# Two attention layers with experts between them on one core: unrolled experts, halved stores, a second DMA queue, sums in PSUM

## The chip, the cores and the metric

One core of a Trainium2 chip runs the whole program in one launch. The metric is the device time of an execution in microseconds (us). PE is TensorE, DVE VectorE, ACT ScalarE, POOL GpSimd and SP SyncE.

## The reference

Four layers follow each other, each added to its input and then normalised over 128 features:

```
x = layernorm(x + attention0(x))   # 16 x 256 tokens, 16 heads of 64, a window mask
x = layernorm(x + experts(x))      # 16 experts 128 -> 512 -> 128, gelu, the best 4 per token, softmax weights
x = layernorm(x + attention1(x))   # 16 heads of 8, weights plus a rank-16 correction
x = layernorm(x + gates(x))        # c = f*c + i*g over the 16 batches, h = tanh(x wo + c_final uo + bo)
```

The gated recurrence runs over the batches, so its last state c_final is known only at the end, and every output row needs it.

## The kernel before, in words

**First attention** (to 667 us). A batch has 256 tokens in two tiles and eight steps `p`. A batch's normalised rows `x1c` are scattered one batch later to a DRAM table `xs`, sorted by expert, by eight indirect DMAs that POOL issues, two per step; the row numbers `pos` come from a chain of small DVE operations behind the routing.

**Experts.** 144 tiles of 128 sorted rows. For each, SP loads rows (`xg<-xs`), PE turns them and multiplies by `wA`, ACT applies gelu, PE multiplies by `wB`, DVE adds the bias, and SP stores to `ys`. 24 tiles make a turn; the first two turns and the last stand written out, three run in a loop. The semaphore `a_done` holds all engines at the start until each has ended the first attention.

**Second attention.** Iteration `b` works on several batches at once: scores and softmax of batch b, score maxima for b+1, queries and keys for b+2, normalisation for b+3, fetches of expert results (`yk<-ys`, eight indirect DMAs per batch, POOL) for b+5, gates for b-2. Queries and keys are split into three bf16 parts; SP stores them (`qkd<-parts`), and reads them back as ten loads, in rows of 4096 bf16 (8 KB), the stack `qst`/`kst` (one of three stacks lies in `wall`, so that loads show as `wall<-qkd`). Row maxima of the first 8 heads are ready at step 5, of the other 8 at step 1 of the next iteration: PE turns them, ACT copies them to `mrow`, SP copies `mrow` eight times into the stack (`qst<-mrow`, `wall<-mrow`, L459). PE's transposed scores (L892) of steps 0 and 4 wait for the two copies. Then ACT takes exponentials (L1086) from one pair of PSUM tiles, PE multiplies with the values (L904).

**End.** When the last state is known PE forms c_final uo (L994), DVE and POOL add it and `bo2` to all 16 batches' outputs in SBUF (L1477, L677), ACT takes tanh (L1151), then four groups of eight tiles are summed, normalised and stored, the last scaling on ACT (L1156).

The order on each engine is that in which the code is written; PE, for example, takes the score products (`scores`) of step 7 after turning the next batches' rows.

Of the kernel before, what the change touches and what calls it, by code (L numbers as in the profile page):

```python
# [10 lines left out]
ALU = mybir.AluOpType  # L11
# [18 lines left out]
GT = 128  # L30
# [3 lines left out]
TURN = 24  # L34
# [67 lines left out]
def build(nc, t, out):  # L102
    ctx = ExitStack()
    with ctx:
# [3 lines left out]
        def sem(name):  # L108
# [147 lines left out]
        state = sb("state", [128, TT, D])  # L256
# [15 lines left out]
        qkd = nc.dram_tensor("qkd", (2, NPART, 128, N), bf16, kind="Internal").ap()  # L272
# [7 lines left out]
            ksq_ready rmat_ready a_done plan_ready zrow_ready plan_out plan_in filled  # L280
# [3 lines left out]
            yk_in0 yk_in1 gates_in weighed comb_done var2_ready pow2_ready posc_ready state_mm state_ready h_pre h_pre_last last_sum var3_ready pow3_ready scale_ready h_act fin_ready out_done""".split()  # L284
# [26 lines left out]

        def group(c):

            return [x[:, 8 * c:8 * c + 8, :].rearrange("q (k i) d -> q k i d", i=TT) for x in (xo_all, x_all)]

        def per_batch(v):
            return v[:, :, :].rearrange("q (o i) d -> q o i d", o=1).to_broadcast([128, 4, TT, D])
# [41 lines left out]
        def _(sp):  # L359
# [39 lines left out]
            sp.wait_ge(s["a_done"], 4)  # L399

# [14 lines left out]

            for n in range(4):
                load_rows(n, n)
# [8 lines left out]
            batch_loop(sp, 2, NT // TURN - 1, 2, body)  # L426
# [3 lines left out]
            def attention(b, par):  # L430
                if has(b, 0):
                    spread_maxima(b, TMB, par, 1)
                if has(b, 2):
                    load = (par + 2) % 3
                    need_alone(sp, "parts_ready", b + 3)

                    need_alone(sp, "stk", 16 * NSTK * (b + 2))
                    for w in range(2):
                        sp.dma_start(qkd[w].rearrange("a r n -> r a n"), parts[:, :, w * N:(w + 1) * N]).then_inc(s["qkd_out"], 16)
                    need_alone(sp, "qkd_out", 32 * (b + 3))  # L440

                    need_alone(sp, "st_full", 8 * b)
                    rows = qkd.rearrange("w a (d h) n -> w (a d) h n", h=H1)
                    n = 0
                    for qa in range(NPART):
                        count = NPART - qa
                        sp.dma_start(kst[load][DH1 * n:DH1 * (n + count), :, :], rows[1, 0:DH1 * count, :, :]).then_inc(s["stk"], 16)
                        for k in range(count):
                            sp.dma_start(qst[load][DH1 * (n + k):DH1 * (n + k + 1), :, :], rows[0, DH1 * qa:DH1 * (qa + 1), :, :]).then_inc(s["stk"], 16)
                        n += count  # L450
                    sp.dma_start(qst[load][MROW:MROW + NMAX, :, :], no_maxima).then_inc(s["stk"], 16)
                if has(b, 1):
                    spread_maxima(b, TMA, (par + 1) % 3, 0)

            def spread_maxima(b, use, slot, half):

                need_alone(sp, f"free{use[0]}", tally[use[0]].before(b, use[1] + 1))
                hh = H1 // 2
                sp.dma_start(qst[slot][MROW:MROW + NMAX, half * hh:half * hh + hh, :],  # L459
                             mrow[:, half, :].rearrange("q (o n) -> q o n", o=1).to_broadcast([NMAX, hh, N])).then_inc(s["mrow_in"], 16)  # L460

            no_maxima = zeros.bitcast(bf16).rearrange("(q h) n -> q h n", h=H1)
# [3 lines left out]
            for c in range(B // 4):  # L466
                sp.wait_ge(s["fin_ready"], c + 1)
                sp.dma_start(out[c * 4 * N:(c + 1) * 4 * N, :].rearrange("(n p) d -> p n d", p=128), x_all[:, 8 * c:8 * c + 8, :]).then_inc(s["out_done"], 16)
            sp.wait_ge(s["out_done"], 16 * B // 4)

        @block.gpsimd
        def _(pool):
# [25 lines left out]
            def body(b):  # L498
                for p in range(8):
# [3 lines left out]
                    if p == 4 and is_batch(b, -1):  # L503
# [3 lines left out]
                    if p == 5 and is_batch(b, -1):  # L507
                        need(pool, "x1c_ready", b)
                        g.tensor_copy(x_all[:, bass.ds((b - 1) * TT, TT), :], x1c[:, :, :]).then_inc(s["x1_kept"], 1)
                    if p < 4 and is_batch(b, -2):  # L510
# [3 lines left out]
                        for k in (2 * p, 2 * p + 1):  # L514
                            nc.gpsimd.indirect_dma_start(  # L515
                                out=xs, out_offset=bass.IndirectOffsetOnAxis(pos[:, k:k + 1], 0),
                                in_=x1c[:, k // TOPK, :], in_offset=None).then_inc(s["scat"], 16)
# [84 lines left out]
            def fetch(b, par, half):  # L602

                if has(b, 5):
                    slot, count = (par + 2) % 3, TT * TOPK // 2
                    need_alone(pool, f"yk_in{half}", 16 * count * (b + 5))
                    if half == 0:
                        need_alone(pool, "comb_done", b + 3)
                        g.tensor_copy(gcur[:, slot, :], gate_all[:, bass.ds(b + 5, 1), :].rearrange("q o k -> q (o k)")).then_inc(s["gates_in"], 1)
                    first = bass.ds((b + 5) * TT * TOPK + count * half, count)  # L610
                    g.tensor_copy(posc[:, half, :], pos_all[:, first]).then_inc(s["posc_ready"], 1)
                    need_alone(pool, "posc_ready", 2 * (b + 5) + (half + 1))
                    for n in range(count):
# [32 lines left out]
            def new_state(b):  # L646

                if has(b, -2):
# [7 lines left out]
                    g.tensor_tensor(c2[:, :], c2[:, :], tg[:, :], ALU.add).then_inc(s["scan_done"], 1)  # L656

# [9 lines left out]
            for b in range(-5, 2):  # L667
                outputs(b, b % 3)
# [6 lines left out]
            xo, xt = group(GROUPS - 1)  # L675
            pool.wait_ge(s["state_ready"], 1)
            g.tensor_tensor(xo, xo, per_batch(state), ALU.add).then_inc(s["h_pre_last"], 1)  # L677
            for c in range(GROUPS):
                if c == 1:
                    pool.wait_ge(s["h_act"], GROUPS)  # L680
                    g.tensor_tensor(xt, xt, xo, ALU.add).then_inc(s["last_sum"], 1)
# [4 lines left out]
        def _(pe):  # L686
# [125 lines left out]
            def after_attention(b, p):  # L812

                if p == 5:
# [3 lines left out]
                    for it in range(TT):  # L818
                        last = nc.tensor.transpose(M[:, it * 128:(it + 1) * 128], x1c[:, it, :], ident[:, :])
# [23 lines left out]
            pe.wait_ge(s["a_done"], 4)  # L843
# [10 lines left out]
            rows_in(1, 1, 16)  # L854
            def tiles(i):
                for p in range(TURN):
                    n, two = TURN * i + p, p % 2
                    if is_tile(i, p, 0):
# [3 lines left out]
                        for f in range(FC):  # L862
                            at = (f // 2) * 512 + (f % 2) * GT
                            mm(UP[two][:, at:at + GT], wA[:, p % 4, f * 128:(f + 1) * 128], xgT[:, p % 4, :], start=True, stop=True).then_inc(s["up_mm"], 1)  # L864
                    if is_tile(i, p, 2):
# [10 lines left out]
            batch_loop(pe, 2, NT // TURN - 1, 2, tiles)  # L876
# [5 lines left out]
            def attention(b, par):  # L882
                nxt = (par + 1) % 3
                for p in range(8):
# [22 lines left out]
                    if p == 4 and has(b, -2):  # L907
                        need(pe, "scan_done", b - 1)
                        need_x2T_x3T(pe, b)
                        gates(b, GA)  # L910
                    if p == 6 and has(b, -2):
# [26 lines left out]
                    if p == 3 and has(b, -1):  # L938
# [4 lines left out]
                        last.then_inc(s[f"full{WO[0]}"], 1)  # L943
                    if p == 7 and (has(b, 3) or has(b, -1)):
# [11 lines left out]
                    scores(b, p, nxt)  # L956
# [32 lines left out]

            attention_loop(pe, attention)  # L990
# [566 lines left out]
```

## Time and profile before

| | |
|---|---|
| median of 3 runs | 1532.71 us (1528.11 to 1534.6) |
| profiled execution | 1530.1 us, of which the span of its instructions is 1528.3 us |
| mean granted clock of TensorE | 0.93 |
| PE busy | 1270.1 us (83% of the span) |
| DVE, ACT, POOL busy | 1011.6, 939.1, 796.6 us |

Times in rows are us from the start of the span. A row of the timeline is start, length, engine, line of the code, operation, `out<-in`, shape and number of instructions merged; in brackets stands how long the engine was idle before it and what ended that. The granted clock is 1.0 for 2.4 GHz and 0.5 for 1.2 GHz.

### The profile page before, as it was taken

The numbers are of one execution on the slowest core, as the hardware profiler recorded it, in microseconds if no ns is written. First come the engines' busy times: TensorE is split into PE (matmuls) and PEld (weight loads), VectorE is DVE, ScalarE is ACT, GpSimd is POOL, SyncE is SP. The second block draws the span as 40 slices with busy tenths as digits, with TensorE's granted clock in tenths as the row PEclk, the third lists the DMA queues.
The fourth block names the chain that finished last, engine by engine and source line by source line (L and its number), as shares of the span: only waits on it lengthen the run. The fifth ranks groups of instructions, "written<-read, shape, count | busy, mean of one in ns | idle before, by whom it ended". The sixth has DMA issues, their size and how long they took to land.

```text
span 1528.3 us, 36861 instructions
## 1 busy us (share of the span) xinstructions
PE 1270.1 (83%) x9712; PEld 970.9 (64%) x9712; DVE 1011.6 (66%) x3751; ACT 939.1 (61%) x2828; POOL 796.6 (52%) x1025
## 2 busy tenths in 40 slices
PE   7999999999999999856999889803768787878870
PEld 3776767777777776646999889801445554555540
DVE  2677777777777777755776657514677776668726
ACT  5877777777777777624665456412555655656544
POOL 1557777777777777743332100175456665653133
PEclk9999999999999999978999999955899999999995
DMA  9522222222222222112222122115343435343201
GB/s 345 171 60 70 69 67 67 69 69 69 69 69 69 69 69 69 44 51 58 72 69 70 58 61 70 56 45 92 82 86 74 94 66 91 68 88 57 46 4 55
DMA packets 150448, 115.51 MB, mean 76 GB/s; under 512 B 11809, under 2 KB 139937, under 8 KB 148290
## 3 DMA queue, kind: packets, MB, share of 16 engines
q1 hardware_dynamic: 142146, 97.50, 24.9%
q0 software_dynamic: 8192, 16.79, 4.2%
q8 instruction: 39, 0.64, 0.2%
q14 instruction: 71, 0.58, 0.1%
HBM read 50.02 MB, written 61.08 MB: 73 GB/s over the span
## 4 chain that ended last, share of the span: by engine, by line
PE 29%; DMA 7%; DVE 5%; issue 4%; DVEq 3%; POOL 2%; ACT 2%; another core or an unknown queue 2%; SPq 1%; POOLq 1%; ACTq 0%
PE psum L864 8%; PE psum L873 8%; DMA qst<-mrow 3%; DMA wall<-mrow 3%; PE psum L904 2%; PE psum L892 2%; PE psum L967 2%; POOL yk L614 1%; PE psum L983 1%; PE psum L850 1%; DVE mx L1389 1%; PE psum L984 1%; ACT wall L1086 1%; DMA yk<-ys,posc 1%
## 5 line engine op out<-in xcount | busy, mean ns | idle before, releaser
L525 POOL TENSOR_SCALAR P<-P,rinv 128x192 f32<-128x192 f32 (+1 forms) x384 | 309.4, 820 | 154.1 <-DVE rinv L1216 151.7
L1051 ACT ACTIVATE P<-shifted,least 128x192 f32<-128x192 f32 (+1 forms) x512 | 240.2, 471 | 103.2 <-DVE least L1202 101.8
L1076 ACT ACTIVATE hid<-psum,wA 128x128 f32<-128x128 f32 x576 | 164.7, 369 | 118.9 <-PE psum L864 118.9
L1389 DVE TENSOR_REDUCE mx<-psum 128x2 f32<-128x512 f32 x256 | 165.0, 686 | 83.4 <-PE psum L967 56.1
L1086 ACT ACTIVATE wall<-psum 128x1024 f32<-128x1024 f32 x128 | 131.1, 1024 | 98.9 <-PE psum L892 81.7
L1202 DVE CUSTOM_DVE_ANT_0 shifted<-psum,band 128x192 f32<-128x192 f32 (+1 forms) x512 | 168.7, 384 | 26.0 <-PE psum L749 25.7
L864 PE MATMUL psum<-xgT,wA 128*128 128x128 f32 x1152 | 155.8, 279 | 8.9 <-DVE xgT L1355 8.8
L515 POOL DMA_INDIRECT xs<-x1c,pos x128 | 128.2, 1001 | 56.8 <-issue 28.3
L873 PE MATMUL psum<-wB,hid 128*128 128x128 f32 x1152 | 153.5, 277 | 0.0
L614 POOL DMA_INDIRECT yk<-ys,posc x128 | 124.2, 970 | 55.7 <-issue 29.0
L864 PEld LDWEIGHTS psum<-xgT,wA 128*128 128x128 f32 x1152 | 143.4, 196 | 9.6 <-issue 9.5
L873 PEld LDWEIGHTS psum<-wB,hid 128*128 128x128 f32 x1152 | 141.5, 194 | 0.0
L786 PEld LDWEIGHTS psum<-ident,P 128*128 128x128 f32 x1024 | 117.0, 141 | 36.3 <-issue 29.4
L786 PE MATMUL psum<-ident,P 128*128 128x128 f32 x1024 | 134.9, 274 | 3.7 <-POOL P L525 1.5
L749 PE MATMUL psum<-kT,qT 64*128 64x192 f32 (+1 forms) x1024 | 131.5, 375 | 0.6 <-DVE least L1202 0.6
L804 PE MATMUL psum<-PT,V 128*64 128x256 f32 (+1 forms) x1024 | 112.2, 362 | 0.7 <-DVE PT L1190 0.7
L749 PEld LDWEIGHTS psum<-kT,qT 64*128 64x128 f32 x1024 | 80.2, 186 | 38.6 <-issue 36.9
L1348 DVE COPY wA<-wall 128x516 f32 x144 | 61.9, 430 | 64.4 <-ACT hid L1076 41.5
L1051 ACT ACTIVATION_READ_ACCUMULATOR P<-shifted,least 128x1 f32 x512 | 95.9, 187 | 0.0
L1190 DVE COPY PT<-psum 128x448 f32<-128x448 f32 x128 | 79.0, 618 | 17.1 <-PE psum L804 7.8
L697 PE MATMUL psum<-hT,wg 128*128 (+1 forms) x256 | 88.9, 429 | 1.7 <-ACT kT L1008 0.9
L804 PEld LDWEIGHTS psum<-PT,V 128*64 128x64 f32 x1024 | 68.5, 138 | 30.9 <-issue 9.0
(243 smaller groups left out, 2550.7 us busy)
## 6 DMA issues: line engine op xcount, KB each, us to landing
xs<-zrow SPq DMA_DIRECT2D x33, 1024.0 KB
xg<-xs SPq DMA_DIRECT2D x144, 64.0 KB, 1.8
ys<-yrow SPq DMA_DIRECT2D x72, 128.0 KB, 1.9
wall<-in_wall SPq DMA_DIRECT2D x1, 8232.0 KB, 36.5
qkd<-parts SPq DMA_DIRECT2D x32, 192.0 KB
qst<-qkd SPq DMA_DIRECT2D x66, 64.0 KB
wall<-qkd SPq DMA_DIRECT2D x35, 64.0 KB
kst<-qkd SPq DMA_DIRECT2D x11, 192.0 KB
```

The costliest lines, as they stand in the source:

```text
L525: g.tensor_scalar(x, x, rinv[:, par, n:n + 1], None, ALU.mult).then_inc(s["pn_ready"], 1)
L614: g.indirect_dma_start(out=yk[:, slot, count * half + n, :], out_offset=None, in_=ys, in_offset=bass.IndirectOffsetOnAxis(posc[:, half, n: ...
L749: last = mm(bk[:, c0:c0 + w], qT[64 * h:64 * h + 64, p, it * 128:(it + 1) * 128], kT[64 * h:64 * h + 64, p, 0:w], start=True, stop=True)
L786: last = nc.tensor.transpose(bk[:, c0:c0 + 128], P[:, par1, it, h, jt * 128:(jt + 1) * 128], ident[:, :])
L804: last = mm(OTB[64 * h:64 * h + 64, k * N + c0:k * N + N], V[:, jt, r * 128 + 64 * h:r * 128 + 64 * h + 64], PT[:, k, h, keys], start=(jt ...
L864: mm(UP[two][:, at:at + GT], wA[:, p % 4, f * 128:(f + 1) * 128], xgT[:, p % 4, :], start=True, stop=True).then_inc(s["up_mm"], 1)
L873: last = mm(DN[two][:, 0:D], hid[:, m, f, :], wB[:, m, f * D:(f + 1) * D], start=(f == 0), stop=(f == FC - 1))
L1051: last = sc.activation(P[:, par, it, h, 0:w], shifted[:, par, it, h, 0:w], ACT.Exp, scale=-1.0, bias=least[:, par, n:n + 1], accum_out=row ...
L1076: sc.activation(hid[:, p % 4, f, :], UP[two][:, at:at + GT], ACT.Gelu, bias=wA[:, p % 4, F + f:F + f + 1]).then_inc(s["hid_ready"], 1)
L1086: sc.activation(pc[:, p % 4, :, :, :].rearrange("q h j n -> q (h j n)"), ST, ACT.Exp, scale=SCALE1).then_inc(s["exps1"], 1)
L1202: v.tensor_tensor_reduce(out=shifted[:, par, it, h, 0:w], in0=bk[:, c0:c0 + w], in1=band[:, it, 0:w], scale=-SCALE0, scalar=3.0e38, op0=AL ...
L1389: v.tensor_reduce(out=mx[:, :, h], in_=SB[(par + 1 + h) % 3].rearrange("q (i n) -> q i n", i=TT), axis=mybir.AxisListType.X, op=ALU.max).t ...
```

## The change

It joins five edits: the experts' turns are all written out (a turn is 8 tiles); the parts are stored by halves of 64 partitions, heads 0 to 7 and 8 to 15, and read back as two pieces of 4 KB per partition; the copies of maxima are issued by ACT; the last state is added on PE, in PSUM, where the outputs are put by a product with the identity; and several waits and orders between the stages are changed. The core of the diff:

```diff
-TURN = 24
+TURN = 8
+        def rows_of(b):
+            return h1[:, 0, :].rearrange("q (i d) -> q i d", d=D)[:, 0:TT, :] if isinstance(b, int) and b == B - 1 else x1c
...
-            sp.wait_ge(s["a_done"], 4)
+            first_rows = [row_of(n) for n in range(4)]
+            sp.wait_ge(s["scat"], 16 * B * TT * TOPK)
             for n in range(4):
-                load_rows(n, n)
+                sp.dma_start(xg[:, n, :], xs[bass.ds(first_rows[n], GT), :]).then_inc(s[f"xg_in{n}"], 16)
...
-            batch_loop(sp, 2, NT // TURN - 1, 2, body)
+            for i in range(NT // TURN + 1):
+                body(i)
...
                     for w in range(2):
-                        sp.dma_start(qkd[w].rearrange("a r n -> r a n"), parts[:, :, w * N:(w + 1) * N]).then_inc(s["qkd_out"], 16)
+                        for e in range(2):
+                            sp.dma_start(qkd[w, e].rearrange("a r n -> r a n"), parts[64 * e:64 * e + 64, :, w * N:(w + 1) * N]).then_inc(s["qkd_out"], 16)
...
-                    if p == 4 and is_batch(b, -1):
+                    if p == (3 if isinstance(b, int) and b == B else 4) and is_batch(b, -1):
                         need_alone(pool, "var_ready", b)
                         g.tensor_tensor(rstd[:, :], veps[:, :], minus_half[:, 0:TT], ALU.pow).then_inc(s["pow_ready"], 1)
...
+                if has(b, -2):
+                    need_alone(pool, f"free{GB[0]}", tally[GB[0]].before(b, GB[1] + 1))
+                    g.tensor_tensor(xo, xo, bo2[:, :].rearrange("q (o d) -> q o d", o=1).to_broadcast([128, TT, D]), ALU.add).then_inc(s["xo_kept"], 1)
...
+            fetch(-4, -4 % 3, 0, 0, 2)
+            combine(-4, -4 % 3)
+            fetch(-4, -4 % 3, 0, 2, 3)
+            deviations(-3)
...
+                    if p == 5 and isinstance(b, int) and b == B:
+                        outputs_in(0)
+                        outputs_in(1)
...
+                    scores(b, p, nxt)
                     if p == 7 and (has(b, 3) or has(b, -1)):
...
-                    scores(b, p, nxt)
...
             attention_loop(pe, attention)
             pe.wait_ge(s["scan_done"], B + 1)
-            for it in range(TT):
-                last = mm(SB[0][:, it * D:(it + 1) * D], c2[:, it * 128:(it + 1) * 128], gu[:, 3, :], start=True, stop=True)
+            state_in(0)
+            state_in(1)
+            outputs_in(3)
+            state_in(2)
+            state_in(3)
...
+            sc.activation(sqj[:, 0:1], ident[:, 0:1], ACT.Gelu)
...
             def maxima_row(b, use, slot, half):
                 need_full(act, b, use)
                 sc.activation(mrow[:, half, :], shared(use).bitcast(bf16)[0:NMAX, 0:N], ACT.Copy).then_inc(s[f"free{use[0]}"], 1)
+                need_alone(act, f"free{use[0]}", tally[use[0]].before(b, use[1] + 1))
+                act.dma_start(qst[slot][MROW:MROW + NMAX, half * hh:half * hh + hh, :],
+                              mrow[:, half, :].rearrange("q (o n) -> q o n", o=1).to_broadcast([NMAX, hh, N])).then_inc(s["mrow_in"], 16)
...
-                        need(dve, "scat", 16 * TT * TOPK * (b - 1))
+                        if not (isinstance(b, int) and b == B):
+                            need(dve, "scat", 16 * TT * TOPK * (b - 1))
...
+                    if p == 7 and isinstance(b, int) and b >= B:
+                        dve.wait_ge(s["gate_act"], b - 1)
+                        v.scalar_tensor_tensor(tf[:, :], tf[:, :], 1.0, c2[:, :], ALU.add, ALU.mult)
+                        v.scalar_tensor_tensor(tg[:, :], ti[:, :], 1.0, tg[:, :], ALU.add, ALU.mult)
+                        v.scalar_tensor_tensor(c2[:, :], tf[:, :], 0.5, tg[:, :], ALU.mult, ALU.add).then_inc(s["scan_done"], 1)
...
+                if c == GROUPS - 1:
+                    for k in range(4, 8):
+                        last = v.tensor_scalar(x, x, mv2[:, c, k, 0:1], rstd2[:, c, k:k + 1], ALU.subtract, ALU.mult)
```

Where the text above says heads by halves, the columns of `cwqk` are sorted likewise. On ACT the weighing of the fetched results of the first batches moves behind the first copy of `parts`.

**POOL, start of the second attention, before.** Behind the fetches for batch 0 stand four and four fetches for batch 1 around the sum of batch 0 (L640 to L644), and then the power for batch 0's deviation (L622):

```order
L614 DMA yk<-ys,posc 128x128 [waits posc_ready]
L614 DMA yk<-ys,posc 128x128 x3
L640 TENSOR_TENSOR yk<-yk 128x2x256 [waits weighed]
L642 TENSOR_TENSOR sums<-yk 128x256
L644 TENSOR_TENSOR sums<-sums,x_all 128x256
L611 COPY posc<-pos_all 128x4 [waits yk_in1]
L614 DMA yk<-ys,posc 128x128 [waits posc_ready]
L614 DMA yk<-ys,posc 128x128 x3
L622 TENSOR_TENSOR rstd<-ve,minus_half 128x2 [waits var2_ready]
```

The same place in the changed kernel:

```order
L611 DMA yk<-ys,posc 128x128 [waits posc_ready]
L611 DMA yk<-ys,posc 128x128
L637 TENSOR_TENSOR yk<-yk 128x2x256 [waits weighed]
L639 TENSOR_TENSOR sums<-yk 128x256
L641 TENSOR_TENSOR sums<-sums,x_all 128x256
L611 DMA yk<-ys,posc 128x128
L619 TENSOR_TENSOR rstd<-ve,minus_half 128x2 [waits var2_ready]
```

Three fetches instead of eight stand ahead of the power.

**ACT, step 5 of the last iterations of the second attention, changed kernel.** The copy to `mrow` is followed by the DMA, which waits until that copy is written (`free1`); before, the next exponential stood there:

```order
L1150 ACTIVATE wall<-psum 128x1024 [waits pv_full,st_full]
L1206 ACTIVATE mrow<-psum 24x256 [waits full1]
L1209 DMA qst<-mrow 24x8x256 [waits free1]
L1150 ACTIVATE wall<-psum 128x1024 [waits pv_full,st_full]
L1154 ACTIVATE oTc<-psum 128x256 [waits to_full,pv_full]
```

In the loop the weighing of fetched results (four activations) stands between the DMA and that exponential.

**PE, the end, before**, from the last gates (L983 with `x3T`, L984 with the state `c`) to the state's product:

```order
L983 MATMUL psum<-x3T,gw 128x256 [waits free1,free0,scan_done]
L984 MATMUL psum<-c,gu 128x256
L983 MATMUL psum<-x3T,gw 128x256
L984 MATMUL psum<-c,gu 128x256
L983 MATMUL psum<-x3T,gw 128x256 [waits free0]
L984 MATMUL psum<-c,gu 128x256
L987 MATMUL psum<-gw,x3T 128x128 x2
L994 MATMUL psum<-gu,c 128x128 [waits scan_done]
L994 MATMUL psum<-gu,c 128x128
```

and in the changed kernel:

```order
L1017 MATMUL psum<-x3T,gw 128x256 [waits free1,free0]
L1017 MATMUL psum<-x3T,gw 128x256 [waits free1]
L1017 MATMUL psum<-x3T,gw 128x256 [waits free0]
L1019 MATMUL psum<-gw,x3T 128x128 x2
L1041 MATMUL psum<-wall,ident 128x512 [waits o_free,to_free,max_done,xo_kept]
L1041 MATMUL psum<-wall,ident 128x512
L1023 MATMUL psum<-c,gu 128x256 [waits scan_done]
L1023 MATMUL psum<-c,gu 128x256 x2
L1048 MATMUL psum<-gu,c 128x2x128 [waits scan_done]
L1048 MATMUL psum<-gu,c 128x2x128 x7
L1041 MATMUL psum<-wall,ident 128x512 [waits free1,free0,xo_kept]
L1041 MATMUL psum<-wall,ident 128x512
```

The products with `x3T` now stand ahead of the wait for the state (`scan_done`), with one pair of identity products (L1041) between; four more such products stand earlier, between the gates of the batch before.

## Rows read from the trace of the kernel before

**Rows 1.** Second attention: length, busy PE, PEld, DVE, ACT, POOL, clock, DMA share, GB/s.

```profile
1068.00:1470.00 402.00, 320.81 (x2674) 213.29 (x2674) 282.01 (x854) 236.23 (x461) 202.96 (x275) 0.93 0.37 72
```

**Rows 2.** Timeline, PE, where the experts' loop returns to its start.

```profile
839.63 1.06 PE L873 MATMUL psum<-wB,hid 128*128 128x128 f32 x8
845.34 2.07 PE L864 MATMUL psum<-xgT,wA 128*128 128x128 f32 x8 [4.66 <-DVE xgT L1355]
...
897.23 1.93 PE L864 MATMUL psum<-xgT,wA 128*128 128x128 f32 x8 [4.10 <-DVE xgT L1355]
```

**Rows 3.** Timeline, DVE at the end of the first attention.

```profile
674.41 0.60 DVE L1262 TENSOR_SCALAR x1c<-res,mv,rstd 128x128 f32<-128x128 f32 x2 [0.52 <-DMA xs<-x1c,pos]
```

**Rows 4.** The chain that ended last, first attention to experts (start, length, what).

```profile
692.10 2.23 DMA xs<-x1c,pos
694.35 1.31 POOLq L529
697.90 1.69 DMA xg<-xs
```

**Rows 5.** Timeline, several engines, from the experts to the second attention.

```profile
1018.60 0.16 DVE L94 TENSOR_TENSOR u<-rstd 128x2 f32<-128x2 f32 x1 [5.26 <-POOL rstd L622]
...
1026.05 1.28 ACT L1136 ACTIVATE yk<-yk,gcur 128x128 f32<-128x128 f32 x4 [2.01 <-DMA yk<-ys,posc]
...
1030.87 0.38 SPq L447 DMA_DIRECT2D kst<-qkd  x1
...
1033.70 0.94 POOL L614 DMA_INDIRECT yk<-ys,posc  x1 [0.30 <-issue]
...
1043.62 1.28 ACT L1136 ACTIVATE yk<-yk,gcur 128x128 f32<-128x128 f32 x4 [16.29 <-DMA yk<-ys,posc]
1044.01 1.04 PE L967 MATMUL psum<-kst,qst 128*128 128x256 bf16 x4 [6.40 <-DMA qst<-zeros]
```

**Rows 6.** Line L459: issue (ns min/median/max) and who waited for it (us, times).

```profile
L459 SPq DMA_DIRECT2D qst<-mrow x22: 778/818/992, 1058.2 to 1456.6; - x22
...
  PE psum L892: 36.4, 10
```

**Rows 7.** Timeline, SP, ACT and PE, copies of maxima, second attention.

```profile
1067.94 1.04 PE L892 MATMUL psum<-qst,kst 128*128 128x256 bf16 x4 [6.90 <-DMA qst<-mrow]
...
1266.52 16.25 SPq L459 DMA_DIRECT2D wall<-mrow  x2
...
1274.27 1.02 ACT L1086 ACTIVATE wall<-psum 128x1024 f32<-128x1024 f32 x1 [1.06 <-remote]
...
1276.54 1.03 PE L892 MATMUL psum<-wall 128*128 128x256 bf16 x4 [2.65 <-DMA wall<-mrow]
1277.50 1.94 PE L904 MATMUL psum<-wall,v 128*32 128x256 f32 x16
...
1432.06 1.03 PE L892 MATMUL psum<-wall 128*128 128x256 bf16 x4 [4.93 <-DMA wall<-mrow]
...
1447.93 9.41 SPq L459 DMA_DIRECT2D qst<-mrow  x2
...
1452.84 0.60 PE L892 MATMUL psum<-qst,kst 128*128 128x256 bf16 x4 [0.33 <-ACT wall L1086]
```

**Rows 8.** Timeline, ACT, the exponential behind step 5's weighing.

```profile
1323.33 1.02 ACT L1086 ACTIVATE wall<-psum 128x1024 f32<-128x1024 f32 x1 [1.30 <-PE psum L892]
```

**Rows 9.** Timeline, the end.

```profile
1489.42 0.41 POOL L650 TENSOR_SCALAR tf<-tf 128x256 f32<-128x256 f32 x1 [5.75 <-ACT tg L1112]
...
1493.11 1.22 PE L994 MATMUL psum<-gu,c 128*128 128x128 f32 x4 [4.40 <-POOL c L656]
...
1498.36 4.28 ACT L1151 ACTIVATE wall<-wall 128x1024 f32<-128x1024 f32 x4 [8.85 <-DVE wall L1477]
1500.52 1.21 DVE L1484 TENSOR_TENSOR x_all<-x_all,wall 128x1024 f32<-128x1024 f32 x1
...
1518.43 6.26 ACT L1156 ACTIVATE x_all<-x_all,shift,rstd 128x128 f32<-128x128 f32 x16 [0.20 <-DVE shift L1493]
```

More of the change, by code:

```diff
@@ L310, in build @@
         GROUPS = B // 4
[L312 to L317, printed above, removed]
         def has(b, off):
@@ L646, in new_state @@
             def new_state(b):
-                if has(b, -2):
+                if has(b, -2) and not (isinstance(b, int) and b >= B):
                     need_alone(pool, "gate_act", b - 1)
@@ L874, in tiles @@
                         last.then_inc(s["dn_mm"], 1)
-            batch_loop(pe, 2, NT // TURN - 1, 2, tiles)
+            for i in range(NT // TURN + 1):
+                tiles(i)
             pe.wait_ge(s["c_set"], 1)
@@ L988, in gates, with last_gates @@
                 last.then_inc(s[f"full{use[0]}"], 1)
+            def last_gates(b):
+                need_x2T_x3T(pe, b)
+                parts = (GA, 0, 0), (GA, 1, 1), (GB, 0, 2)
+                for use, n, k in parts:
+                    need_free(pe, b, use)
+                    mm(shared(use)[:, n * N:(n + 1) * N], gw[:, k, :], x3T[:, :], start=(n == 0), stop=False)
+                for it in range(TT):
+                    mm(shared(GB)[:, N + it * D:N + (it + 1) * D], x3T[:, it * 128:(it + 1) * 128], gw[:, 3, :], start=False, stop=False)
+                outputs_in(2)
+                need(pe, "scan_done", b - 1)
+                for use, n, k in parts:
+                    last = mm(shared(use)[:, n * N:(n + 1) * N], gu[:, k, :], c2[:, :], start=False, stop=(n == 1 or use == GB))
+                    if n == 1 or use == GB:
+                        last.then_inc(s[f"full{use[0]}"], 1)
@@ L1076, in tiles @@
                             sc.activation(hid[:, p % 4, f, :], UP[two][:, at:at + GT], ACT.Gelu, bias=wA[:, p % 4, F + f:F + f + 1]).then_inc(s["hid_ready"], 1)
-            batch_loop(act, 2, NT // TURN - 1, 2, tiles)
+            for i in range(NT // TURN + 1):
+                tiles(i)
             def attention(b, par):
@@ L1125, in attention @@
                         last.then_inc(s[f"free{TX[0]}"], 1)
-                    if p == 7 and isinstance(b, int) and b == -3:
-                        for half in range(2):
-                            weigh(b, par, half)
             def weigh(b, par, half):
@@ L1341, in _ @@
             dve.wait_ge(s["plan_in"], 16)
+            dve.wait_ge(s["b2_kept"], E // 4)
             def expert_of(n):
@@ L1359, in _ @@
                 weights_A(first, n)
+                weights_B(first, n)
+            for n in range(2):
                 rows_T(n, n)
-                weights_B(first, n)
             def tiles(i):
@@ L1379, in tiles @@
                         weights_B(e, q)
-            batch_loop(dve, 2, NT // TURN - 1, 2, tiles)
+            for i in range(NT // TURN + 1):
+                tiles(i)
             def row_maxima(b, p, par):
```

196 lines of the change are left out of this document (111 added, 85 removed).

## Prediction

> **What bounds the kernel now.** I read the table of stretches, then the chain that ended last, then the timeline at each place that the change touches. PE is busy for 320.81 of the second attention's 402 us [rows 1], and for all but two gaps of the experts; the rest of the time is lost where a stage hands over to the next. Five places matter.
>
> *Experts' loop.* Tiles follow each other every 1.9 us, except that after the tile at 839.63 PE stands idle for 4.66 us and then multiplies at half clock (2.07 us instead of 1.06 for eight products); the same follows at 897.23 with 4.10 [rows 2]. Both places are the loop's return to its start.
>
> *First attention to experts.* The last rows are normalised at 674.41, after DVE has waited 0.52 us for the scatter of the batch before [rows 3]. The last scatter lands at 694.33, then comes POOL's drain (1.31) and the reading of row numbers, so that the second load of rows starts only at 697.90 [rows 4].
>
> *Experts to second attention.* POOL issues fetches at 1.24 us each (0.94 and 0.30 of idle). DVE waits 5.26 us for a power that stands behind them in POOL's order; the first stack of keys is loaded from 1030.87 on, and PE waits for its last part until 1044.01 [rows 5].
>
> *Second attention.* In ten iterations PE waits for the copy of maxima, 36.4 us in all [rows 6]. The copy issued at 1266.52 arrives at 1276.54, 10.0 us later; without stack loads around it the one of 1447.93 was there by 1452.84, so within 4.9 us [rows 7]. The burst of stack loads stands ahead of it in SP's queue.
>
> *End.* The state is ready at 1493.11, but DVE begins the first sum only at 1500.52, since the state is first added to all outputs, and ACT's last 16 scalings begin at 1518.43 and take 6.26 us [rows 9].
>
> **The change part by part**, against the profiled execution's own 1530.1 us, which is 0.17% under the median.
>
> *Experts written out.* Both gaps go: idle 4.66 and 4.10, and after each about two groups of eight products that took 1.01 and 0.87 us more than at full clock [rows 2]: 8.76 + 2.02 + 1.74 = 12.5. The turns that are already written out keep the 1.9 us beat, which is why I charge nothing for more code. Bounds: 11 (only the idle and one slow group each) to 13. **-12.5.**
>
> *To the experts.* The power for the last batch moves ahead of two scatters: 2 x 1.24 = 2.5, if a scatter costs what a fetch does. With a buffer of its own the last batch needs no wait for a scatter: 0.5 [rows 3]. Its `pos` is written ahead of three small operations: about 0.4. The eight last scatters thus start 3.4 earlier. Behind them SP waits for the scatters alone, with its row numbers read: between landing (694.33) and second load (697.90) lie 3.57 us [rows 4], of which I take 2.6, since the first load, which started earlier, is now what the first tile needs. The gelu table is loaded early, but PE hardly waited for it: nothing. Bounds 4.5 to 7. **-6.0.**
>
> *To the second attention.* Ahead of batch 0's power stand three fetches instead of eight: 5 x 1.24 = 6.2, and one copy of positions with its wait less, about 1. ACT does `parts` before it weighs the next batch. Against that SP issues two more stores: 0.5. The whole chain (power, x2T, queries, parts, stack) moves with it, since nothing else ends later than it there: PE had waited 6.40 us for the stack [rows 5]. Bounds 4 to 8.5. **-6.7.**
>
> *Second attention, copy of maxima.* Two prices are unknown. First, what a queue of its own saves. Nothing is the one end; the other is that the copy then takes 4.9 us or less, as without loads, and all removable waiting goes. Not all 36.4 are removable: at 1276.54 ACT had ended the exponential before only at 1275.29, so 1.2 of the 2.65 could go; read in the same way all ten (from 6.9 at 1067.94 to 4.7 of 4.93 at 1432.06) come to 26.5 [rows 6, 7]. Also, seven of the nine later waits are followed by scores at 1.03 instead of about 0.6 us and by L904 at 1.94 instead of about 1.1 [rows 7]: half clock, 1.4 us each, up to 9.8. Between the ends the nearest row is POOL's: the fetch issued at 1033.70, in a queue of its own, beside a burst of stack loads, was used only at 1043.62, 9.9 us later, when the loads ended too; ACT waited 16.29 us for it, and 2.01 for the one fetched ahead of the burst [rows 5]. So a queue of its own gave next to nothing while pieces were 8 KB. Pieces of 4 KB let another queue in twice as often, if queues take turns; I take a quarter of the way from 10.0 to 4.9, some 1.2 us per copy: 11.1 over the ten (two waits allow less), and two half-clock starts avoided: 2.8.
>
> By the Trainium skill (DMA: Bandwidth & Descriptors, "Queues, rings and completion order") SP and ACT have rings of their own on the same 16 DMA engines, and an engine goes round between the rings packet by packet; the fetch above, which shared no queue with the loads and yet ended with them, agrees with the shared engines, and no run here shows the size of a turn.
>
> Second, what an issue costs on ACT. SP's took 0.82 us in the median [rows 6], and ACT must also wait for its own write. At step 5 ACT stood idle for 1.30 us before the next exponential [rows 8], which covers an issue and a short wait; where that idle is not there, the exponential is late, and PE's next L892 with it. I take 0.2 us of each of 32 issues: 6.4. Bounds: nothing, and 32 x 0.82 = 26.2. POOL's addition of `bo2` and the moved scores I count at nothing: POOL is idle for half of this stretch (202.96 of 402 busy [rows 1]), and if that cover were gone, the next fetch would be late, needed a batch later. The SP queue loses its waits for ACT, but these hid nothing: it waits for `parts` next. **-11.1 - 2.8 + 6.4 = -7.5.**
>
> *End.* Up to the state I see no gain: DVE's three steps replace POOL's five (1489.42 to 1493.11, 3.7 us [rows 9]) twice, but six identity products come in on PE around the last gates. After it, PE must add the state to one group: L994's two products took 1.22 us at half clock, four of twice the width some 3.4 (estimate); with one tanh (4.28/4 = 1.07 [rows 9]) DVE starts 4.6 instead of 7.4 us after the state: -2.8. DVE scales four of the last 16 tiles, so ACT's last stretch falls from 6.26 to 4.7; DVE's part overlaps: -1.3. Bounds +1 (identity products on the path) to -8. **-4.1.**
>
> Sum: -12.5 - 6.0 - 6.7 - 7.5 - 4.1 = -36.8, so 1530.1 - 36.8 = **1493 us**.
>
> **Rivals.**
> 1. *The queue of its own gives nothing*: the copy still lands with the burst, as POOL's fetch did, while ACT pays 6.4. The second attention comes out at +6.4 instead of -7.5: 1507 us. For it: rows 5; against it: the shorter pieces.
> 2. *It frees the copy*: 26.5 and most of 9.8 us go, less 6.4: about -29 instead of -7.5: 1472 us. For it: 4.9 us without loads [rows 7]; against it: rows 5.
> 3. *Slower*: ACT's issue holds exponentials. All other terms give 43.2; to lose that over 32 issues each must expose 1.35 us, so more than the whole 0.82 that SP needs. To be slower by 8 us it must be 1.6: 1538 us. Only a far longer issue on ACT does that; no row speaks for it.
> 4. *The gaps are not the loop's*: if code that is fetched anew made them, they would stay, and 12.5 are lost: 1505 us. Against it: the written-out turns show none.
>
> The Trainium skill (same page, "Rules for kernel authors") says that spreading DMAs over issuing engines doesn't help bandwidth, and that two transfers to halves of the partitions aren't worth it; that is rival 1, 1507 us, and the fetch of rows 5 agrees with it so far.
>
> **How the numbers follow.** Forecast (1484 to 1500) 0.42, rival 2 with values up to it 0.24, rival 1 with 4 0.26, rival 3 0.03, no or hardly any change 0.05. The range reaches from a little under rival 2 (1467) to a little over rival 1 (1512). A measurement of this kernel tells about 0.5% (8 us) from no change: rivals 1, 2 and 4 all lie beyond it, so faster 0.92, same 0.05, slower 0.03.
>
> **What would show it.** Experts: no PE idle over 2 us between 705 us and the end of the tiles, 1.9 us per tile. To the experts: first load some 6 us earlier, no SP wait on POOL's drain. To the second attention: from the end of the experts to the first stack's use 7 us less. Copy of maxima: from ACT's issue to the waiting L892 about 8.8 us; 10 is rival 1, 5 is rival 2; idle of ACT ahead of step 6's exponential near zero. End: from the last state to DVE's first sum under 5 us. The prediction falls if the second attention as a whole (402 us) changes by over 20 us either way, or if the gaps at the tiles stay.

## The result, and the profile after

| | before | after |
|---|---|---|
| median | 1531.7 us | 1512.67 us (1510.52 to 1514.89) |
| profiled execution, span of its instructions | 1528.3 us | 1509.9 us |
| mean granted clock of TensorE | 0.930 | 0.938 |

The ratio is 0.9877 (95% interval 0.985 to 0.9904): faster by 19 us, where 37 were forecast. The forecast was 1493 us and its range ended at 1512.

I cut both spans at the same events: the first product with `wA`, the end of the last product with `wB`, the first transposed scores (L892 before, L907 now) of batches 0 and 15, and the end.

| stretch (us) | before | after | change | forecast |
|---|---|---|---|---|
| start to the first expert product | 700.0 | 691.4 | -8.5 | -6.0 |
| experts' tiles | 287.9 | 276.3 | -11.6 | -12.5 |
| end of the tiles to batch 0's scores | 80.0 | 72.5 | -7.5 | -6.7 |
| batch 0 to batch 15 | 384.9 | 401.4 | **+16.5** | **-7.5** |
| batch 15 to the end | 75.5 | 68.3 | -7.2 | -4.1 |
| sum | 1528.3 | 1509.9 | -18.4 | -36.8 |

Four stretches came out as forecast or a little better, and one went the other way by 24 us.

The timeline of PE in the changed kernel, where the loop used to return. Lines 2 and 4 are the tiles that stood behind the two gaps of [rows 2]:

```profile
831.42 1.06 PE L876 MATMUL psum<-xgT,wA 128*128 128x128 f32 x8
833.32 1.06 PE L876 MATMUL psum<-xgT,wA 128*128 128x128 f32 x8
...
876.92 1.06 PE L876 MATMUL psum<-xgT,wA 128*128 128x128 f32 x8
878.82 1.06 PE L876 MATMUL psum<-xgT,wA 128*128 128x128 f32 x8
```

The tiles keep their 1.9 us; from 831 to 881 us PE is busy throughout at a granted clock of 1.00. The idle times of 4.66 and 4.10 us and the half-clock groups are gone.

The timeline at the end of the first attention (DVE, POOL and SP; answers to [rows 3, 4]):

```profile
667.13 0.75 POOL L502 TENSOR_TENSOR rstd<-veps,minus_half 128x2 f32<-128x2 f32 x1
668.06 1.03 POOL L511 DMA_INDIRECT xs<-x1c,pos  x1 [0.18 <-issue]
...
668.63 0.60 DVE L1329 TENSOR_SCALAR h<-res,mv,rstd 128x128 f32<-128x128 f32 x2
...
685.89 0.96 POOL L511 DMA_INDIRECT xs<-h,pos  x1 [0.30 <-issue]
688.67 1.95 SPq L413 DMA_DIRECT2D xg<-xs  x4
```

The power now stands ahead of two scatters, the rows need no wait, and SP starts its four loads 2.8 us after the last scatter's issue.

The timeline from the experts to the second attention (PE and ACT; answers to [rows 5]):

```profile
992.83 0.66 PE L972 MATMUL psum<-ident,x2c 128*128 128x128 f32 x2 [25.08 <-DVE x2c L1505]
...
1017.55 0.66 PE L972 MATMUL psum<-ident,x2c 128*128 128x128 f32 x2 [21.51 <-DVE x2c L1505]
1018.05 1.03 PE L988 MATMUL psum<-kst,qst 128*128 128x256 bf16 x4
...
1040.26 1.04 PE L907 MATMUL psum<-qst,kst 128*128 128x256 bf16 x4 [0.38 <-DMA qst<-mrow]
...
1043.78 1.28 ACT L1200 ACTIVATE yk<-yk,gcur 128x128 f32<-128x128 f32 x4 [11.35 <-DMA yk<-ys,posc]
...
1046.65 1.02 ACT L1150 ACTIVATE wall<-psum 128x1024 f32<-128x1024 f32 x1
...
1070.32 1.04 PE L907 MATMUL psum<-qst,kst 128*128 128x256 bf16 x4 [3.31 <-DMA qst<-mrow]
```

The same two sets of turned rows in the kernel before:

```profile
1020.07 0.66 PE L950 MATMUL psum<-ident,x2c 128*128 128x128 f32 x2 [32.17 <-DVE x2c L1434]
...
1036.95 0.66 PE L950 MATMUL psum<-ident,x2c 128*128 128x128 f32 x2 [13.67 <-DVE x2c L1434]
```

The tiles end at 967.75 us, and at 987.90 before. So the first turned rows come 7.1 us sooner after the tiles (25.1 for 32.2 us), but the next batch's do not (49.8 for 49.1). Batch 0's scores stand at 1040.26. But ACT waits 11.35 us for a fetch, a table load of 1.28 us stands behind the weighing, and the exponential of these scores begins only at 1046.65. Batch 0's iteration takes 30.1 us; before it took 24.8 (1067.94 to 1092.73). Three batches on, nothing of the gain is left: from the tiles' end to batch 3's scores it is 158.3 us against 157.7.

SP's timeline in one iteration (batch 4, which starts at 1153.62), and the start of batch 5:

```profile
1164.30 2.13 SPq L435 DMA_DIRECT2D qkd<-parts  x4
1168.64 0.30 SPq L444 DMA_DIRECT2D kst<-qkd  x1
1168.98 0.99 SPq L446 DMA_DIRECT2D qst<-qkd  x3
...
1171.30 0.80 ACTq L1209 DMA_DIRECT2D wall<-mrow  x1
1171.74 0.39 SPq L448 DMA_DIRECT2D qst<-zeros  x1
...
1181.97 0.82 PE L907 MATMUL psum<-wall 128*128 128x256 bf16 x4 [2.12 <-DMA wall<-mrow]
```

From the first store to the first load lie 4.34 us. ACT's copy is issued 2.7 us behind the first load and ends PE's wait 10.7 us later. Line L1209 as a whole (issue in ns, min/median/max, and who waited; answers to [rows 6]):

```profile
L1209 ACTq DMA_DIRECT2D qst<-mrow x22: 803/804/1442, 1029.6 to 1445.8; - x22
L1209 ACTq DMA_DIRECT2D wall<-mrow x10: 803/804/823, 1088.2 to 1426.9; - x10
...
  PE psum L907: 25.2, 9
```

The nine batch starts that waited for it began 9.0 to 10.7 us after ACT's issue, 9.9 in the mean: rival 1's 10, not the forecast's 8.8. The packets of the copies (192 of 512 bytes each), which the traces hold one by one, say the same. Beside a burst of loads, a copy's last packet ended 8.0 us after ACT's issue (mean of 15 copies, 4.1 to 9.9); in the kernel before it was 8.1 after SP's (6.4 to 9.5). Without loads it was 2.3 and 2.2. The waiting fell by 11.2 us all the same (36.4 to 25.2), the sum that I had charged. That is luck, since the copies came no sooner; and the stretch still grew.

The timeline of the end (answers to [rows 9]):

```profile
1480.04 3.72 PE L1048 MATMUL psum<-gu,c 128*128 128x256 f32 x16 [2.52 <-DVE c L1544]
1482.07 1.03 ACT L1217 ACTIVATE wall<-psum 128x1024 f32<-128x1024 f32 x1 [3.47 <-PE psum L1048]
1483.20 1.23 DVE L1552 TENSOR_TENSOR x_all<-x_all,wall 128x1024 f32<-128x1024 f32 x1 [3.21 <-ACT wall L1217]
...
1501.22 4.75 ACT L1222 ACTIVATE x_all<-x_all,shift,rstd 128x128 f32<-128x128 f32 x12 [1.47 <-DVE shift L1559]
```

DVE's first sum begins 3.2 us after the state instead of 7.4, and ACT's last stretch takes 4.75 instead of 6.26.

### The profile page after: what moved, and what is told of

Its sections match the earlier page's. It is cut to its first block, busy times and chain, and to the rows that moved or that the text cites. A ratio compares the mean times of both kernels' runs of the same rounds, so it can differ in the third digit from the quotient of the medians.

```text
span 1509.9 us, 36382 instructions
## 1 busy us (share of the span) xinstructions
PE 1282.7 (85%) x9756; PEld 971.6 (64%) x9756; DVE 1012.8 (67%) x3759; ACT 938.1 (62%) x2825; POOL 799.3 (53%) x1029
## 4 chain that ended last, share of the span: by engine, by line
PE 60%; DVE 10%; issue 9%; DMA 6%; ACT 5%; another core or an unknown queue 3%; POOL 3%; DVEq 3%; ACTq 1%; POOLq 0%; SPq 0%
PE psum L876 9%; PE psum L887 8%; PE psum L762 6%; PE psum L799 6%; PE psum L817 6%; PE psum L710 3%; PE psum L919 3%; PE psum L779 3%; PE psum L717 3%; DMA qst<-mrow 3%; PE psum L907 2%; PE psum L711 2%; DMA wall<-mrow 2%; PE psum L988 2%
## 5 line engine op out<-in xcount | busy, mean ns | idle before, releaser
L511 POOL DMA_INDIRECT xs<-x1c,pos x120 | 120.5, 1004 | 39.1 <-issue 34.5
```

## The experiments

Ratios are to the kernel before, with their 95% intervals; 0.001 is 1.5 us. In the expectations, theory A blames ACT's issue of the copies, B the halves, C the order of scores at step 7.

**1. The copies back on SP, from the changed kernel.**

```diff
-                act.dma_start(qst[slot][MROW:MROW + NMAX, half * hh:half * hh + hh, :], ...
+                if has(b, 0):
+                    spread_maxima(b, TMB, par, 1)
...
+                if has(b, 1):
+                    spread_maxima(b, TMA, (par + 1) % 3, 0)
```

The first added call stands ahead of SP's stores, the second behind its loads.

> The changed kernel with the two copies of maxima per batch issued by SP again, at the places they had before; all else as changed. Theory A (the issue on ACT costs more than the own queue gives: in the changed kernel ACT sits idle for 1.09 us between the copy to mrow and the next activation, twice a batch, and the exponential behind it is late): the stretch from the first transposed scores of batch 0 to those of batch 15 falls from 401 to about 387 us, and the time from 1512.7 to about 1499. Theory B (the halves did it: four stores instead of two, two pieces per partition): the stretch stays at 399 to 405 and the time at 1511 to 1516, or rises, since the copies now stand behind the burst in one queue. Theory C (scores taken ahead of the turned rows at step 7): no change.

Measured: 0.9951 (0.992 to 0.9983), 1526.83 us; batch 0 to 15 takes 408.5 us. Theory A falls: with the halves, ACT's queue is worth 11 us.

**2. Parts stored and loaded whole, copies on ACT.**

```diff
-                        for e in range(2):
-                            sp.dma_start(qkd[w, e].rearrange("a r n -> r a n"), parts[64 * e:64 * e + 64, :, w * N:(w + 1) * N]).then_inc(s["qkd_out"], 16)
+                        sp.dma_start(qkd[w].rearrange("a r n -> r a n"), parts[:, :, w * N:(w + 1) * N]).then_inc(s["qkd_out"], 16)
```

with the loads and the columns of `cwqk` as before.

> The changed kernel with the parts stored and loaded whole again (two stores, pieces of 8 KB), copies of maxima still on ACT. Theory A: time within 3 us of 1512.7, the copies still land 9 to 11 us after their issue. Theory B: the stretch from batch 0 to batch 15 falls from 401 towards 387, time about 1499. Theory C: no change.

Measured: 0.9823 (0.9802 to 0.9845), 1507.66 us; batch 0 to 15 takes 387.9 us. The halves cost 8 us. The stretch came as theory B expected, the time 9 us above its 1499.

**3. Both undone.**

> Both undone: copies of maxima on SP and the stack stored and loaded whole, so that the second attention's DMAs are those of the kernel before; order of scores, addition of bo2 on POOL, start and end as changed. Theories A and B both expect the stretch from batch 0 to batch 15 at about 385 to 388 us and a time of 1497 to 1500; if A alone is right it equals the run with the maxima on SP within 3 us, if B alone the run with the whole stack. Theory C: 401 and 1512 stay.

Measured: 0.9842 (0.982 to 0.9864), 1510.16 us; batch 0 to 15 takes 394.7. Beside run 1, the halves cost 17 us when SP also issues the copies; beside run 2, ACT's queue is worth 3 us without halves, within the intervals. Both theories missed here: they expected 385 to 388 and 1497 to 1500 us. With the DMAs of the kernel before, the stretch is still 10 us longer than its 384.9; 5.7 of them lie in batches 0 to 3 (83.4 for 77.7). So halves and queue are not all of the loss.

**4. Scores of step 7 behind the turned rows.**

> The changed kernel with PE's score products of step 7 behind the turned rows again, as before; all else as changed. Theory C: the stretch from batch 0 to batch 15 falls from 401 to about 390 us, time about 1501. Theories A and B: no change beyond 3 us, 1510 to 1516.

Measured: 0.9889 (0.9832 to 0.9947), 1516.43 us, 403.6 for the stretch. No change that can be told; theory C falls.

SP's stores and first load of an iteration, first with the stack whole (run 2):

```profile
1189.83 0.91 SPq L434 DMA_DIRECT2D qkd<-parts  x2
1193.20 0.15 SPq L442 DMA_DIRECT2D kst<-qkd  x1
```

The store to load takes 3.4 us here and took 4.3 in the changed kernel. In the mean over batches 3 to 13 it is 3.38 against 4.81, and 3.14 in the kernel before. This led to theory D: the period is a loop of parts, store, load and a copy that lands with the end of the loads, so that two more stores are paid in each batch. If so, a copy that stands ahead of half the loads must shorten it.

**5. Only the experts written out, from the kernel before.**

```diff
-TURN = 24
+TURN = 8
...
-            batch_loop(pe, 2, NT // TURN - 1, 2, tiles)
+            for i in range(NT // TURN + 1):
+                tiles(i)
```

> The kernel before with the experts' turns written out and nothing else changed. If the prediction's first term is right: 12.5 us less than before (ratio about 0.992), tiles at 1.9 us throughout, no PE idle over 2 us in them. If the gaps come from code that is fetched anew: ratio 0.998 to 1.0, gaps still there.

Measured: 0.9935 (0.9912 to 0.9959), 10 us less; the tiles take 275.2 us instead of 287.9. The first term holds, the rival of code fetched anew falls.

**6. As run 2, one weighing later.**

```diff
+                    if p == 1 and isinstance(b, int) and b == 0:
+                        weigh(-1, -1 % 3, 1)
...
-                        if not (isinstance(b, int) and b < -1):
+                        if not (isinstance(b, int) and (b < -1 or b == -1 and p == 6)):
```

> The changed kernel with the stack stored and loaded whole, and with ACT's weighing of the second half of batch 3's fetched results moved behind step 1 of batch 0, so that batch 0's first exponential no longer stands behind a fetch. If that wait is what gives back the gain of the start: batch 0's iteration falls from 30 to about 25 us and the time from 1507.7 to about 1503. If something else ends last there (the copies of maxima, the loads of the next stack): batch 0's iteration shrinks by under 1.5 us and the time stays at 1506 to 1510.

Measured: 0.9817 (0.9788 to 0.9846), 1508.67 us: as run 2. Batch 0's iteration shrinks from 30.2 to 28.9 us. ACT's timeline shows the wait one batch further on:

```profile
1072.01 1.28 ACT L1200 ACTIVATE yk<-yk,gcur 128x128 f32<-128x128 f32 x4 [4.47 <-DMA yk<-ys,posc]
1075.38 1.02 ACT L1148 ACTIVATE wall<-psum 128x1024 f32<-128x1024 f32 x1 [0.92 <-PE psum L905]
```

**7. Split loads: whole stores, the loads of heads 0 to 7, then the copy by SP, then the loads of heads 8 to 15.**

```diff
+                    half_loads(0)
+                if has(b, 1):
+                    spread_maxima(b, TMA, (par + 1) % 3, 0)
+                if has(b, 2):
+                    half_loads(1)
...
-                if p == 0:
-                    need(pe, "stk", 16 * NSTK * (b + 2))
+                if p % 4 == 0:
+                    need(pe, f"stk{p // 4}", 16 * NSTK * (b + 2))
```

> The changed kernel with whole stores (two per batch), the loads split by heads (first heads 0 to 7 of all parts, then 8 to 15), and SP issuing the copy of maxima between the two halves, so that only half of the burst stands ahead of it. Theory D (the period is a loop: parts, store, start of the burst, copy that lands with the end of the burst, next start of scores; whatever delays the burst's start or lies ahead of the copy lengthens every period): from the load's start to the next batch's start falls from 13.4 to 10 or less, the period from 26 to about 24 us, time about 1485 (1475 to 1495). Rival E (the period is set by the engines, and a wait for the copy only shows where they would wait anyway): period stays at 25.5 to 26.5, time 1503 to 1513.

Measured: **0.9648 (0.962 to 0.9676), 1482.26 us**, 30 us under the changed kernel by the medians, 35 by the ratios. SP's timeline in one iteration:

```profile
1209.67 0.80 SPq L449 DMA_DIRECT2D wall<-qkd  x1
1210.52 0.29 SPq L451 DMA_DIRECT2D wall<-zeros  x1
1211.02 0.85 SPq L462 DMA_DIRECT2D qst<-mrow  x1
1211.92 0.53 SPq L447 DMA_DIRECT2D wall<-qkd  x1
```

PE's waits of batches 3 to 10 in this run (waited for: us in total, times, longest):

```profile
PE psum L1004 <- DVE mx L1470: 17.0, 10, 3.1
PE psum L923 <- ACT wall L1166: 9.8, 11, 1.6
PE psum L1012 <- ACT ti L1192: 7.0, 8, 2.1
```

and in the kernel before, over the same batches:

```profile
PE psum L967 <- DVE mx L1389: 8.2, 9, 2.0
PE psum L892 <- ACT wall L1086: 7.7, 6, 2.1
PE psum L892 <- DMA wall<-mrow: 6.5, 2, 3.9
PE psum L892 <- DMA qst<-mrow: 5.9, 2, 3.7
```

None of PE's products waits for the copy any more in this run (two weight loads do, 2.6 us). A copy's last packet now ends 2.4 us after SP's issue (mean of 15, 2.3 to 3.1), where it took 8.2 with whole loads and SP's copies behind them (run 3). The time met theory D's number, but the place did not: the period of batches 3 to 10 stays at 26.6 us (212.6 over eight), as before (211.7). There DVE's maxima and ACT's activations take the place of the copy, which is rival E; what holds the period while POOL fetches was not tried further. The gain lies at both ends:

| us | tiles' end to batch 0 | batch 0 to 3 | 3 to 11 | 11 to 15 | 15 to end |
|---|---|---|---|---|---|
| before | 80.0 | 77.7 | 211.7 | 95.5 | 75.5 |
| after | 72.5 | 85.8 | 216.2 | 99.4 | 68.3 |
| run 2, whole | 77.8 | 81.9 | 209.0 | 97.0 | 73.3 |
| run 7, split loads | 69.7 | 77.8 | 212.6 | 83.5 | 67.9 |
| run 10, ACT's queue alone | 77.0 | 80.5 | 209.6 | 97.5 | 76.0 |

Each row is one profiled execution; kernels that hardly differ there are some 4 us apart in batches 3 to 11 (216.2 after, 220.0 in run 8). From batch 11 on POOL fetches nothing more; in batches 12 and 13 the period falls to 20.6 and 20.8 us in run 7, where the changed kernel takes 25.3 and 26.2. In the changed kernel PE waits for the copy there:

```profile
1370.04 1.03 PE L907 MATMUL psum<-qst,kst 128*128 128x256 bf16 x4 [4.63 <-DMA qst<-mrow]
...
1395.36 1.04 PE L907 MATMUL psum<-qst,kst 128*128 128x256 bf16 x4 [3.66 <-DMA qst<-mrow]
...
1421.52 1.04 PE L907 MATMUL psum<-wall 128*128 128x256 bf16 x4 [4.00 <-DMA wall<-mrow]
```

and in run 7 it does not:

```profile
1372.33 0.60 PE L923 MATMUL psum<-qst,kst 128*128 128x256 bf16 x4
...
1393.10 0.60 PE L923 MATMUL psum<-wall 128*128 128x256 bf16 x4 [0.33 <-ACT wall L1166]
```

The clock has a share in it: in batches 11 to 15 the granted clock is 1.00 in run 7 and 0.91 in the changed kernel, and 6.8 of the 15.9 us gained there are PE's busy time (76.0 for 82.8).

Run 7 also lets PE begin on a stack when its first half has landed. That is an unlikely rival: PE waited for the loads of a stack once in the changed kernel (2.1 us) and never in runs 2 and 3. A run with the split loads and the copy behind both halves was not made.

The run of 7 and 6 together:

> The run with split loads and the later weighing together. Theory D with the start's theory: about 1480, 4 to 6 us under the run with split loads alone; rival E: 1500 to 1510; if the start's wait is not the weighing's: within 2 us of the run with split loads alone.

Measured: 0.9647 (0.9623 to 0.9671), 1481.24 us: the same as run 7.

**8. No addition of `bo2` on POOL** (the kernel leaves the bias out).

```diff
-                    g.tensor_tensor(xo, xo, bo2[:, :]..., ALU.add).then_inc(s["xo_kept"], 1)
+                    pool.sem_inc(s["xo_kept"], 1)
```

> The changed kernel without POOL's addition of bo2 to a batch's outputs (the bias is left out of the output): one POOL operation of 0.8 us less per batch. Theory F (POOL's added operation delays the fetches and the weighing, and ACT's exponentials stand behind them): from the end of the experts to batch 15 falls from 474 to 468 us or less, time 1503 to 1508. Rival: POOL has room (it is idle for half of this stretch), time 1510 to 1515.

Measured: 0.9869 (0.984 to 0.9899), 1513.77 us: POOL has room, theory F falls.

**9. The start's order as before** (POOL's loop of fetches from the first batch on, ACT's weighing at step 7 of the third iteration before batch 0).

> The changed kernel with POOL's order of fetches and ACT's order of weighing at the start of the second attention as before. If the new order really wins 6 to 7 us that last, the time rises from 1512.7 to about 1519. Theory G (the gain at the start is lost by batch 3, since from the end of the experts to batch 3's scores it takes 157.7 us before and 158.3 in the changed kernel): time within 3 us of 1512.7, and that stretch again at 156 to 161 us, although the first normalised rows come some 7 us later.

Measured: 0.9898 (0.9868 to 0.9928), 1519.29 us, 3 us over the changed kernel by the ratios, whose intervals overlap. The first turned rows are back at 32.0 us after the tiles and the second at 48.8, but batch 0's scores stand at 74.3, only 1.8 later than with the new order (72.5). Tiles' end to batch 3 takes 162.1. Neither theory G's 3 nor the full 6 to 7 is excluded. With split loads:

> Split loads with the copy of maxima between the halves, and the order at the start of the second attention as before. If the bursts of loads are what eats the gain of the start (theory G's cause), the order matters once they are split: 5 to 8 us more than the run with split loads (1482), about 1488. If the new order is worth nothing: 1480 to 1484.

Measured: 0.9669 (0.9648 to 0.969), 1481.89 us: 3 over run 7 by the ratio, nothing by the medians. The order is worth some 3 us, not told from nothing.

**10. ACT's queue alone, from the kernel before** (the edit of run 1 the other way round).

> The kernel before with the copies of maxima issued by ACT and nothing else changed. The prediction's term (minus 11.1 and 2.8 for the copies, plus 6.4 for the issues) gives 7.5 us less, ratio 0.995; rival 1 of the prediction 6.4 more, ratio 1.004; rival 2 some 29 less, ratio 0.981. By the run with the whole stack against the one with the maxima on SP as well I expect 3 to 8 less.

Measured: 1.0016 (0.9999 to 1.0033), 1534.22 us: nothing, or 2.5 us lost. Line of the copies, who waited:

```profile
L1133 ACTq DMA_DIRECT2D qst<-mrow x22: 803/804/1462, 1058.5 to 1459.2; - x22
...
  PE psum L881: 35.1, 12
```

35.1 us of waiting against 36.4 [rows 6]: in a queue of its own the copy still came when the loads did, its last packet 8.2 us after the issue. My expectation of 3 to 8 us less was missed too.

**11 and 12. Four stores, whole loads**, with the copies on ACT and on SP; the edit of the stores beside runs 2 and 3:

```diff
-                        sp.dma_start(qkd[w].rearrange("a r n -> r a n"), parts[:, :, w * N:(w + 1) * N]).then_inc(s["qkd_out"], 16)
+                        for e in range(2):
+                            half = slice(64 * e, 64 * e + 64)
+                            sp.dma_start(qkd[w, :, half, :].rearrange("a r n -> r a n"), parts[half, :, w * N:(w + 1) * N]).then_inc(s["qkd_out"], 16)
```

> The run with the whole stack (loads of 8 KB per partition, columns in the old order, maxima on ACT), with each of its two stores per batch cut into two of 64 partitions. If the stores' number is what the halves cost (store to first load 4.8 us instead of 3.4): ratio 0.986 to 0.989 as the changed kernel (0.9877), store to load 4.5 to 4.9 us. If the loads in two pieces of 4 KB are the cost: ratio 0.981 to 0.984 as the run with the whole stack (0.9823).

> The run with maxima on SP and the whole stack, its two stores per batch cut into four likewise. If the stores' number is the cost: ratio 0.992 to 0.997 as the run with the maxima on SP and halves (0.9951). If the loads' pieces are: 0.982 to 0.987 as without the cut (0.9842).

Measured: 0.9845 (0.9829 to 0.9861), 1512.93 us, and 0.9947 (0.9927 to 0.9966), 1527.84 us. SP's timeline of the second:

```profile
1169.89 2.50 SPq L438 DMA_DIRECT2D qkd<-parts  x4
1174.50 0.32 SPq L446 DMA_DIRECT2D kst<-qkd  x1
```

With the copies on SP the cut of the stores alone brings the halves' whole cost (0.9951 with halves, 0.9842 without). With the copies on ACT it brings 3 of 8 us, and its interval touches both neighbours, so there the pieces of 4 KB may have a share.

## Why the prediction was wrong

**Experts: right.** 11.6 for 12.5, and run 5 shows that it comes from the written-out turns.

**To the experts: right, a little small.** 8.5 for 6.0. The last rows are normalised 5.8 us earlier (674.41 [rows 3] to 668.63), where I had 3.0 for the power and the wait; the edits behind them brought 2.7, where I had 3.0. Of the 5.8, only 3.3 are the power and the wait; the other 2.5 lie earlier, since each batch of the first attention takes 39.35 us instead of 39.54. What shortens it was not tried; I had no term for it.

**To the second attention: the number right by luck, the step wrong.** I wrote that the whole chain moves "since nothing else ends later than it there". Batch 0 did come 7.5 us earlier, but the order of POOL and ACT brings only 1.8 of them (run 9). It brings the first turned rows forward by 7 us; the next batch's rows come no sooner (49.8 for 49.1 us after the tiles). The rest of the 7.5 goes with the stores: 71.5 to 74.9 us to batch 0 in the runs with the new order and four stores, 76.8 to 78.4 in those with two and whole loads; why was not tried. Behind batch 0 stands ACT's 11.35 us of waiting, which run 6 moved on by a batch, where 4.47 are left. By batch 3 nothing remains in the profiles, and in the times some 3 us, not told from nothing (run 9).

**Second attention: the step that failed.** It failed in three places.
- *A queue of its own saves 1.2 us per copy.* Alone it saved nothing (run 10, 35.1 us of waiting against 36.4; last packets 8.2 us after the issue against 8.1) and cost 0 to 5 us, where the forecast said 7.5 less: rival 1, whose mechanism the row of POOL's fetch had shown [rows 5]. I had let the pieces of 4 KB speak against that row without any row for it; with them the last packets ended 8.0 us after ACT's issue, with 8 KB (run 2) 7.7. The Trainium skill (DMA: Bandwidth & Descriptors, "Rules for kernel authors") says that spreading DMAs over engines doesn't help bandwidth and only saves issue time; run 10 agrees.
- *The halves at nothing.* I charged 0.5 us once for two more stores, at the start. SP's stores took 0.41 us each in the median before and 0.61 by halves, and the four stand, with the wait for their landing, ahead of every burst of loads: 4.81 instead of 3.14 us from store to load. That cost 8 us here (run 2; the stores alone 3 in run 11, not told from either end) and 17 with the copies on SP (runs 1, 3, 12). The Trainium skill (the same section) says that two transfers to halves of the partitions aren't worth it; these runs agree.
- *A wait counted as a gain.* The 25.2 us that remain and the 11.2 that went are in part time that PE would have spent waiting for something else. Run 7 takes them all away, and the period of batches 3 to 10 does not move. So in the kernel before, only at the start and from batch 11 on is the copy what ends last.

The stretches of the profiles account for the 24 us by which the second attention missed. The 7.5 for the queue did not come. 8.1 lie in batches 0 to 3, where the start's gain is given back. 8.4 lie in batches 3 to 15, which take 306 to 311 us in all runs with two stores and whole loads (307 before) and 316 to 327 in all with four stores. The ratios agree, with wide margins: queue 4.5 to 10 us off (forecast -7.5; -3 from runs 2 and 3, +2.5 from run 10), halves 8, start up to 7, together 13 to 25, less some 5 by which the other stretches came out better; the miss was 18 by the ratio. The 6.4 for ACT's issues is not told apart from the rest of the queue's. My sign of being wrong, 20 us in the second attention, was set too wide to catch a loss of 16.5.

**End: right, the size low.** 7.2 for 4.1: 5.3 of them behind the state, where 4.1 were worked out, 1.9 ahead of it, where I had seen no gain.

Open is the share of the 4 KB pieces with the copies on ACT, and how much of the start's order lasts; both lie within the intervals.

## What to carry to other kernels

Count a wait as gain only where no other engine ends within the same time; here taking all of them away moved the period at the ends of the stage and not in its middle. What stands ahead of a burst of loads is paid in every round in which the last arrival of that burst is waited for, so price each added store there, and move the small urgent transfer ahead of half the burst instead of giving it another queue.

## What was unexpected of the hardware

A small DMA that ACT issued while SP's loads were under way ended no sooner than one that SP issued behind them: its last packet came 8.0 to 8.2 us after the issue, against 8.1, and 2.3 without loads. Between two half bursts in SP's own queue it took 2.4. The issue itself took 0.80 us on ACT and 0.82 on SP. A store of 64 partitions took SP 0.61 us to issue, one of 128 partitions 0.41.
